# A transformer block on one core: the first norm modulated by halves of d, and a new order of loads and work around it

## The chip, the cores and the metric

The kernel runs on one core of a Trainium2 chip. The core has these engines: TensorE for matrix products (PE in the rows; PEld is its weight load), VectorE (DVE), ScalarE (ACT), GpSimd (POOL), and SyncE (SP), which here issues every DMA on one queue. They run side by side and wait for each other with semaphores. The metric is the time of one execution on the device in microseconds (us), as a median of several runs.

## The reference

The block has a modulated layer norm, a linear layer with a block mask, a gated residual, a second modulated norm, and a gated feed-forward net with 4-bit weights.

```python
mod = (silu(c) @ wmod).reshape(4, 6, 1, 1024)
sa, ca, ga, sb, cb, gb = (mod[:, i] for i in range(6))
ga, gb = ((2 * (g >= 0) - 1) * maximum(abs(g), 0.25) for g in (ga, gb))
h = layernorm(x) * (1 + ca) + sa                # x: (4, 512, 1024)
x = x + ga * (h @ (weight * block_mask).T)      # blocks of 32 x 32, any mask entry > 0 keeps one
h = layernorm(x) * (1 + cb) + sb
x = x + gb * ((silu(h @ w1.T) * (h @ w2.T)) @ w3.T)   # w1, w2: 2752 x 1024, w3: 1024 x 2752
```

All of it is in float32. A product is made of three TensorE products of rounded parts: high x high, high x low, low x high.

## The kernel before

The 2048 rows of x are 16 tiles of 128. The program is written by hand as one list of instructions for each engine, with explicit semaphore waits; nothing reorders them. So an instruction that waits holds up all that stands behind it in its engine's list, DMA issues on SP too.

The stage that the change touches is the first: modulation, the first norm, the masked layer, called attention in the names.

- **Modulation.** `modulation(j)` multiplies silu(c) with piece j of wmod (2 MB each, 12 pieces, 3 buffers; load j waits until piece j - 3 is used). Pieces 0 and 1 give row set 0 (the shift sa), 2 and 3 give row set 1 (the scale ca), 4 and 5 the gate ga, 6 to 11 the second norm's. `copy_rows` (ACT) takes a row set out of PSUM, `turn_mod` (PE) transposes it, `read_mod` (DVE) stores it as per-partition factors.
- **Masks and weights.** The weight matrix and the mask come in four pieces of 1 MB: pieces 0 and 1 are the two halves of d (the contraction) for output columns 0 to 511, 2 and 3 those for columns 512 to 1023. `sum_mask`, `mask_column`, `sum_partitions` (PE), `block_mask` make a mask of blocks for an output half. `mask_weight` on DVE (pieces 1 and 3) or POOL (0 and 2) applies it, `weight_high` (ACT) rounds the high part, `split_weight` (DVE) takes the low part and counts `w_lo`.
- **A tile.** `ln1_sums` and `ln1_factors` (DVE, a root on ACT) give mean and deviation, `norm1` (ACT) the normed tile, `turn1` (PE) transposes it in eight 128 x 128 pieces, `input1` (ACT) modulates the eight pieces and rounds the high part AH, `low_part1` (DVE) takes the low part AL. `attend_half(t, hb)` multiplies tile t with output half hb in 24 products of 512 columns. Then `residual_sum` and `residual_norm` (DVE) gate, add and norm again. For tiles 0 and 1 `set_aside` copies the product out first, because the gate isn't there yet: `gate(0)` (DVE) makes it from pieces 4 and 5, SP stores it to DRAM and loads it back spread over the partitions.
- **x slots.** Tile 5 goes into the slot of tile 1, so its load waits until tile 1's sum is stored; on SP it stands behind the store of tile 1's second norm.
- **Early decode.** ACT decodes the first feed-forward weights between tiles, four lines of 1024 columns at a time (`early_lines`).

PE's list is: mask sums, modulations 0 to 3, `turn1(0)`, `turn1(1)`, WARM = 24 products of the identity matrix (their result is not used), output half 0 of tiles 0 and 1, modulations 4 and 5, output half 1 of tile 0, then tile by tile, with `turn1(t + 1)` ahead of tile t's products. Modulations 6 and 7 stand behind tile 1.

## Time and profile before

| | before |
|---|---|
| median of 3 runs | 1596.86 us (1596.29 to 1597.66) |
| profiled execution | 1598.67 us, its span 1596.6 us |
| PE busy | 1547.7 us, 97% of the span |
| PE weight loads | 1272.2 us, 80% |
| DVE, ACT, POOL busy | 1040.9, 985.9, 10.6 us |
| chain that ended last, by engine | PE 93%, DVE 2%, DMA 2%, ACT 1% |

The profiled execution is one run on its own; its span runs from the first to the last instruction. In a timeline row the bracket names how long the engine had been idle ahead of it, and who ended that. PE busy counts the modelled length of overlapping products, so 97% says that PE was hardly without work and not that it ran at its peak. PEclk is the granted clock of TensorE as a share of 2.4 GHz: it is 1.00 or 0.50 (1.2 GHz), and between them only where a stretch holds both. Some products appear as two records (the 24 warm-up products as x48, a modulation as x32).

### The profile page before, as it was taken

Reading aid. Unit: us, or ns where it says so; the run is one execution under the profiler, and the core shown is the slowest. Engines: PE = TensorE matmul, PEld = TensorE weight load, DVE = VectorE, ACT = ScalarE, POOL = GpSimd, SP = SyncE. Lnnn points to the kernel's source line nnn. Section 1 sums busy time; section 2 is a strip of 40 time slices with the busy share of each in tenths; the row PEclk is TensorE's granted clock in tenths of the full one; section 3 lists DMA queues with packets and bytes.
Section 4 is the critical chain, followed back from the end, with each engine's and each line's share of the span. In section 5 each row is a group of like instructions: output and inputs, shape, how many; then the busy total and the mean of one; then the engine's idle time right before and its main releaser. Section 6 shows DMA issues by size and latency. Waiting matters only on the chain.

```text
span 1596.6 us, 19163 instructions
## 1 busy us (share of the span) xinstructions
PE 1547.7 (97%) x7216; PEld 1272.2 (80%) x7216; DVE 1040.9 (65%) x1496; ACT 985.9 (62%) x1280; POOL 10.6 (1%) x11
## 2 busy tenths in 40 slices
PE   3889999999999999999999999999999999999998
PEld 1667788888888888888888888888888888888887
DVE  3677787555455555456776666666775757867777
ACT  1445666899888888885698978887333433333320
POOL 1100000000000000000000000000000000000000
PEclk9899999999999999999999999999999999999999
DMA  9874521465555544553577777686777958958866
GB/s 369 326 260 156 185 83 64 166 208 178 185 178 166 183 158 158 170 165 125 192 236 224 239 223 237 199 243 185 262 273 267 348 192 301 337 194 300 308 217 208
DMA packets 170091, 345.97 MB, mean 217 GB/s; under 512 B 14728, under 2 KB 65288, under 8 KB 170000
## 3 DMA queue, kind: packets, MB, share of 16 engines
q1 hardware_dynamic: 170000, 344.76, 64.1%
q8 instruction: 57, 0.93, 0.2%
q14 instruction: 34, 0.28, 0.1%
HBM read 249.77 MB, written 94.93 MB: 216 GB/s over the span
## 4 chain that ended last, share of the span: by engine, by line
PE 93%; DVE 2%; DMA 2%; ACT 1%; issue 1%; SPq 0%; DVEq 0%; ACTq 0%
PE ps L1811 10%; PE ps L1813 10%; PE ps L1812 10%; PE ps L1886 9%; PE ps L1885 9%; PE ps L1884 9%; PE ps L1823 9%; PE ps L1822 9%; PE ps L1824 9%; PE ps L1746 3%; PE ps L1747 3%; PE ps L1748 3%; DMA wmod<-wmod 2%; PE ps L1710 2%; PE ps L1693 1%; ACT modulated L867 1%
## 5 line engine op out<-in xcount | busy, mean ns | idle before, releaser
L824 ACT ACTIVATE w_raw<-w_raw 128x1024 f32<-128x1024 f32 x287 | 304.8, 1062 | 9.1
L1811 PE MATMUL ps<-ffn_in_hi,w_hi 128*128 128x512 f32 x688 | 268.6, 390 | 0.0
L1813 PE MATMUL ps<-ffn_in_hi,w_lo 128*128 128x512 f32 x688 | 267.8, 389 | 0.0
L1812 PE MATMUL ps<-ffn_in_lo,w_hi 128*128 128x512 f32 x688 | 267.7, 389 | 0.0
L1884 PE MATMUL ps<-t_hi,s_hi 128*128 128x512 f32 x616 | 239.6, 389 | 0.0
L1885 PE MATMUL ps<-t_lo,s_hi 128*128 128x512 f32 x616 | 239.6, 389 | 0.0
L1886 PE MATMUL ps<-t_hi,s_lo 128*128 128x512 f32 x616 | 239.6, 389 | 0.0
L1822 PE MATMUL ps<-x_m_hi,stream_hi 128*128 128x512 f32 x604 | 235.0, 389 | 0.0
L1823 PE MATMUL ps<-x_m_lo,stream_hi 128*128 128x512 f32 x604 | 235.0, 389 | 0.0
L1824 PE MATMUL ps<-x_m_hi,stream_lo 128*128 128x512 f32 x604 | 235.0, 389 | 0.0
L1043 ACT ACTIVATE s_hi<-s_raw 128x1408 fp32r<-128x1408 f32 x56 | 77.5, 1383 | 230.6 <-DVE s_raw L1541 190.0
L836 ACT ACTIVATE w_raw<-w_raw 128x1024 f32<-128x1024 f32 (+1 forms) x154 | 163.4, 1061 | 4.4
L1101 DVE SCALAR_TENSOR_TENSOR w_raw<-w_raw,w_scale 128x1024 f32<-128x1024 f32 x41 | 50.3, 1226 | 174.9 <-ACT w_raw L824 174.9
L1813 PEld LDWEIGHTS ps<-ffn_in_hi,w_lo 128*128 128x128 f32 x688 | 129.1, 188 | 27.1
L1812 PEld LDWEIGHTS ps<-ffn_in_lo,w_hi 128*128 128x128 f32 x688 | 129.2, 188 | 26.5
L1811 PEld LDWEIGHTS ps<-ffn_in_hi,w_hi 128*128 128x128 f32 x688 | 129.2, 188 | 26.4
L1885 PEld LDWEIGHTS ps<-t_lo,s_hi 128*128 128x128 f32 x616 | 115.6, 188 | 24.2
L1884 PEld LDWEIGHTS ps<-t_hi,s_hi 128*128 128x128 f32 x616 | 115.6, 188 | 23.9
L1886 PEld LDWEIGHTS ps<-t_hi,s_lo 128*128 128x128 f32 x616 | 115.6, 188 | 23.9
L1822 PEld LDWEIGHTS ps<-x_m_hi,stream_hi 128*128 128x128 f32 x604 | 113.4, 188 | 23.7
L1824 PEld LDWEIGHTS ps<-x_m_hi,stream_lo 128*128 128x128 f32 x604 | 113.4, 188 | 23.5
L1823 PEld LDWEIGHTS ps<-x_m_lo,stream_hi 128*128 128x128 f32 x604 | 113.4, 188 | 23.4
(134 smaller groups left out, 2100.4 us busy)
## 6 DMA issues: line engine op xcount, KB each, us to landing
s_raw<-h_d SPq DMA_DIRECT2D x96, 704.0 KB, 5.5
stream_raw<-t_d SPq DMA_DIRECT2D x150, 256.0 KB, 3.5
t_d<-combined SPq DMA_DIRECT2D x106, 256.0 KB, 2.6
wmod<-wmod SPq DMA_DIRECT2D x12, 2048.0 KB, 16.3
t_raw<-w_d SPq DMA_DIRECT2D x88, 256.0 KB, 6.4
w_codes<-w12q SPq DMA_DIRECT2D x41, 512.0 KB, 5.1
h_d<-h_tile SPq DMA_DIRECT2D x44, 256.0 KB, 2.4
h_d<-up_c SPq DMA_DIRECT2D x44, 256.0 KB, 3.3
```

The costliest lines, as they stand in the source:

```text
L824: act.activation(RAWF[r], RAWF[r] if j else RQ[r][:], ACT.Prelu, bias=bias, scale=sign, alpha=slope).then_inc(line_ready, 1)
L836: act.activation(E3[p][0:rows, :], (E3 if j else E3Q)[p][0:rows, :], ACT.Prelu, bias=bias, scale=sign, alpha=slope).then_inc(w3_line, 1)
L1043: act.activation(SH[p][:], SR[p][:, 1], ACT.Copy).then_inc(s_hi, 1)
L1811: pe.matmul(acc, RH[r][:, k, :], HH[:, b, k, :], start=(k == 0), stop=False)
L1812: pe.matmul(acc, RH[r][:, k, :], HL[:, b, k, :], start=False, stop=False)
L1813: last = pe.matmul(acc, RL[r][:, k, :], HH[:, b, k, :], start=False, stop=(k == C - 1))
L1822: pe.matmul(acc, th[:, k, :], xh[:, k, :], start=(first and k == 0), stop=False)
L1823: pe.matmul(acc, th[:, k, :], xl[:, k, :], start=False, stop=False)
L1824: last = pe.matmul(acc, tl[:, k, :], xh[:, k, :], start=False, stop=(stop and k == HALF_C - 1))
L1884: pe.matmul(acc, SH[p][:, k, :], TH[place(i)][k][:], start=(k == 0), stop=False)
L1885: pe.matmul(acc, SH[p][:, k, :], TL[place(i)][k][:], start=False, stop=False)
L1886: last = pe.matmul(acc, SL[p][:, k, :], TH[place(i)][k][:], start=False, stop=(k == HC - 1))
```

## The change

What it does:

- The columns of wmod for sa and ca are sorted anew on the host: modulation pieces 0 and 1 now give shift and scale for the first half of d (row set 0), pieces 2 and 3 for the second (row set 1). `read_mod` writes two parts for each.
- Tiles 0 and 1 are turned, modulated, rounded and multiplied by halves of d: `half_turn1`, `half_input1`, `half_low_part1`, `attend_first`. A part is 12 products. Each waits for its weight piece and its half of the input.
- The loads stand in another order: mask pieces 0 and 1, modulation 0 and 1, weight 0, modulation 2 and 3, weight 1, masks 2 and 3, weights 2 and 3, then x tiles 2 and 3, modulation 4 and 5. The early decode's load waits for all four weight pieces in place of two.
- Masks 2 and 3 are summed behind the inputs of the first two tiles. DVE applies the mask to pieces 0, 1 and 2, POOL to piece 3 alone.
- Norms of tiles 2, 3 and 4 stand together ahead of the loop; `gate(0)` stands behind `set_aside(1)`; modulations 6 and 7 behind tile 2. WARM is 16.

`whole(t)` in the diff is t - 1, since tiles 0 and 1 no longer count on the tile semaphores; `weight_at(j)` is j + 1.

```diff
-                    sp.wait_ge(w_lo, 2)
+                    sp.wait_ge(w_lo, 4)
...
-            for j in range(4):
-                load_mask(j)
-            for j in range(3):
-                load_wmod(j)
+            load_mask(0)
+            load_mask(1)
+            load_wmod(0)
+            load_wmod(1)
             load_weight(0)
+            load_wmod(2)
             load_wmod(3)
-            for j in range(1, 4):
-                load_weight(j)
-            load_wmod(4)
-            load_wmod(5)
+            load_weight(1)
+            load_mask(2)
+            load_mask(3)
+            load_weight(2)
+            load_weight(3)
             sp.wait_ge(mask_step, MASK_STEPS + 2)
             load_x(2)
             load_x(3)
+            load_wmod(4)
+            load_wmod(5)
             load_x(EXTRA)
             load_wmod(6)
             load_early(0)
...
-            for j in (0, 2):
-                pool.wait_ge(mask_step, MASK_STEPS * (j // 2 + 1))
-                pool.wait_ge(weight_loaded[j], 16)
-                w4, m4 = masked_views(j)
-                pool.tensor_tensor(w4, w4, m4, ALU.mult).then_inc(piece_masked[0], 1)
+            pool.wait_ge(mask_step, 2 * MASK_STEPS)
+            pool.wait_ge(weight_loaded[3], 16)
+            w4, m4 = masked_views(3)
+            pool.tensor_tensor(w4, w4, m4, ALU.mult).then_inc(piece_masked[0], 1)
...
+            def half_input1(half, t):
+                e = 2 * half + t
+                cs = slice(HALF_C * half, HALF_C * (half + 1))
+                act.wait_ge(half_turned, 2 * t + half + 1)
+                if t:
+                    act.wait_ge(half_low1, e)
+                for c in range(HALF_C * half, HALF_C * (half + 1)):
+                    ins = act.activation(HM[0][:, c, :], ps[:, 4 + half, (c % 4) * P:(c % 4 + 1) * P], ACT.Identity,
+                                         bias=MODS[0][:, batch_of(t), c:c + 1], scale=MODS[0][:, batch_of(t), C + c:C + c + 1])
+                ins.then_inc(half_modulated1, 1)
+                act.wait_ge(half_modulated1, e + 1)
+                act.activation(AH[t][:, cs, :], HM[0][:, cs, :], ACT.Copy).then_inc(half_high1, 1)
...
+            act.wait_ge(mod_read, 2)
+            half_input1(0, 0)
+            half_input1(0, 1)
             copy_rows(1)
             weight_high(1)
-            act.wait_ge(mod_read, 2)
-            input1(0)
-            input1(1)
+            act.wait_ge(mod_read, 4)
+            half_input1(1, 0)
+            half_input1(1, 1)
             weight_high(2)
             weight_high(3)
             for t in range(TILES):
                 if t == 1:
+                    start1(3)
                     input1(2)
-                    start1(3)
+                    start1(4)
+                    input1(3)
                     root(1, 0)
...
+                    elif t > 2 and t + 1 < TILES:
...
-                if t + 2 < TILES and t != 1:
+                if t + 2 < TILES and t not in (1, 2):
...
+            def half_low_part1(half, t):
+                cs = slice(HALF_C * half, HALF_C * (half + 1))
+                dve.wait_ge(half_high1, 2 * half + t + 1)
+                dve.tensor_tensor(AL[t][:, cs, :], HM[0][:, cs, :], AH[t][:, cs, :].bitcast(F32), ALU.subtract).then_inc(half_low1, 1)
...
+            mask_weight(0)
+            read_mod(0)
+            split_weight(0)
+            half_low_part1(0, 0)
+            half_low_part1(0, 1)
+            mask_weight(1)
+            read_mod(1)
+            split_weight(1)
+            half_low_part1(1, 0)
             sum_mask(2)
+            half_low_part1(1, 1)
             sum_mask(3)
             mask_column(1)
             block_mask(1)
-            read_mod(0)
-            mask_weight(1)
-            split_weight(0)
-            read_mod(1)
-            split_weight(1)
-            low_part1(0)
-            mask_weight(3)
-            low_part1(1)
+            mask_weight(2)
             split_weight(2)
             split_weight(3)
...
+            ln1(2)
+            ln1(3)
+            set_aside(0)
+            low_part1(2)
+            set_aside(1)
+            gate(0)
+            ln1(4)
+            low_part1(3)
+            residual_sum(0)
+            residual_norm(0)
+            for t in range(2, TILES):
+                residual_sum(t - 1)
+                if 2 < t < TILES - 2:
+                    ln1_sums(t + 2)
...
+            def half_turn1(half, t):
+                pe.wait_ge(normed1, t + 1)
+                if t:
+                    pe.wait_ge(half_modulated1, 2 * half + 1)
+                for c in range(HALF_C * half, HALF_C * (half + 1)):
+                    last = pe.transpose(ps[:, 4 + half, (c % 4) * P:(c % 4 + 1) * P],
+                                        XN[t][:].rearrange("t (p c) -> t c p", c=C)[:, c, :], IDENT[:])
+                last.then_inc(half_turned, 1)
...
+            half_turn1(0, 0)
+            half_turn1(1, 0)
             modulation(0)
             modulation(1)
             turn_mod(0, 0)
+            for _ in range(WARM):
+                pe.matmul(ps[:, 2, 0:P], IDENT[:], IDENT[:], start=True, stop=True)
+            half_turn1(0, 1)
+            attend_first(0, 0, 0)
             modulation(2)
+            attend_first(1, 0, 0)
             modulation(3)
             turn_mod(1, 1)
-            turn1(0)
-            for t in range(TILES):
-                if t == 0:
-                    turn1(1)
-                    for _ in range(WARM):
-                        pe.matmul(ps[:, 7, 0:P], IDENT[:], IDENT[:], start=True, stop=True)
-                    pe.wait_ge(w_lo, 2)
-                    attend_half(0, 0)
-                    attend_half(1, 0)
-                    modulation(4)
-                    modulation(5)
-                    pe.wait_ge(w_lo, 4)
-                    attend_half(0, 1)
-                else:
-                    if t + 1 < TILES:
-                        turn1(t + 1)
-                    if t in (4, 7):
-                        turn_mod(t // 3 + 2, t // 3 + 1)
-                    if t > 1:
-                        attend_half(t, 0)
-                    attend_half(t, 1)
-                for j in {1: (6, 7), 5: (8, 9), 8: (10, 11)}.get(t, ()):
+            half_turn1(1, 1)
+            attend_first(0, 0, 1)
+            attend_first(1, 0, 1)
+            sum_partitions(1)
+            attend_first(0, 1, 0)
+            attend_first(0, 1, 1)
+            turn1(2)
+            attend_first(1, 1, 0)
+            attend_first(1, 1, 1)
+            modulation(4)
+            modulation(5)
+            for t in range(2, TILES):
+                if t + 1 < TILES:
+                    turn1(t + 1)
+                if t in (4, 7):
+                    turn_mod(t // 3 + 2, t // 3 + 1)
+                attend_half(t, 0)
+                attend_half(t, 1)
+                for j in {2: (6, 7), 5: (8, 9), 8: (10, 11)}.get(t, ()):
...
+    first = a["L0_wmod"][:, :2 * D].reshape(D, 2, P, 2, C // 2).transpose(0, 3, 2, 1, 4).reshape(D, 2 * D)
```

`attend_first(t, hb, half)` waits for `w_lo` of piece 2 * hb + half and for that half's low part, and issues the 12 products of it.

PE's list, from its start to the first attention products. `wmod` is a modulation piece, `normed_186` and `normed_187` are tiles 0 and 1, the products of `identity` alone the warm-up. Before:

```order
L1757 MATMUL ps<-mask_column,four_partition_groups 128x16 x2
L1693 MATMUL ps<-wmod_57,silu_c 4x256 x16
L1693 MATMUL ps<-wmod_58,silu_c 4x256 x16
L1702 MATMUL ps<-identity,mod_rows_193 128x4 x8
L1693 MATMUL ps<-wmod_59,silu_c 4x256 x16
L1693 MATMUL ps<-wmod_57,silu_c 4x256 x16
L1702 MATMUL ps<-identity,mod_rows_193 128x4 x8
L1710 MATMUL ps<-identity,normed_186 128x128 x8
L1710 MATMUL ps<-identity,normed_187 128x128 x8
L1772 MATMUL ps<-identity 128x128 x24
L1746 MATMUL ps<-attn_w_hi,attn_in_hi_78 128x512
```

Now, to the first attention product:

```order
L1829 MATMUL ps<-mask_column,four_partition_groups 128x16
L1770 MATMUL ps<-identity,normed_186 128x128 x8
L1744 MATMUL ps<-wmod_57,silu_c 4x256 x16
L1744 MATMUL ps<-wmod_58,silu_c 4x256 x16
L1753 MATMUL ps<-identity,mod_rows_193 128x4 x8
L1838 MATMUL ps<-identity 128x128 x16
L1770 MATMUL ps<-identity,normed_187 128x128 x4
L1804 MATMUL ps<-attn_w_hi,attn_in_hi_78 128x512
```

Tile 0 is turned ahead of the modulations, half of tile 1 behind the warm-up, and the attention products begin ahead of modulations 2 and 3.

DVE's list around the second output half. `mask_piece_62` and `_63` are masks 2 and 3, `weight_piece_66` and `_67` weights 2 and 3. Before:

```order
L1279 TENSOR_REDUCE mask_column<-mask_sums 128x16
L1284 TENSOR_SCALAR block_mask<-ps 128x16
L1272 TENSOR_REDUCE mask_sums<-mask_piece_62 128x4x16
L1272 TENSOR_REDUCE mask_sums<-mask_piece_63 128x4x16
L1279 TENSOR_REDUCE mask_column<-mask_sums 128x16
L1284 TENSOR_SCALAR block_mask<-ps 128x16
L1142 TENSOR_SCALAR mod_352<-ps 128x4x8
L1290 TENSOR_TENSOR weight_piece_65<-weight_piece_65,block_mask 128x2048
L1294 TENSOR_TENSOR attn_w_lo<-weight_piece_64,attn_w_hi 128x4x512
L1142 TENSOR_SCALAR mod_352<-ps 128x4x8
L1294 TENSOR_TENSOR attn_w_lo<-weight_piece_65,attn_w_hi 128x4x512
L1211 TENSOR_TENSOR attn_in_lo_80<-modulated_188,attn_in_hi_78 128x1024
```

Now:

```order
L1343 TENSOR_TENSOR attn_w_lo<-weight_piece_65,attn_w_hi 128x4x512
L1256 TENSOR_TENSOR attn_in_lo_80<-modulated_188,attn_in_hi_78 128x512
L1321 TENSOR_REDUCE mask_sums<-mask_piece_62 128x4x16
L1256 TENSOR_TENSOR attn_in_lo_81<-modulated_188,attn_in_hi_79 128x512
L1321 TENSOR_REDUCE mask_sums<-mask_piece_63 128x4x16
L1328 TENSOR_REDUCE mask_column<-mask_sums 128x16
L1333 TENSOR_SCALAR block_mask<-ps 128x16
L1339 TENSOR_TENSOR weight_piece_66<-weight_piece_66,block_mask 128x2048
L1343 TENSOR_TENSOR attn_w_lo<-weight_piece_66,attn_w_hi 128x4x512
L1343 TENSOR_TENSOR attn_w_lo<-weight_piece_67,attn_w_hi 128x4x512
```

The mask sums of pieces 2 and 3 moved from ahead of all weights to between and behind the low parts of the second half of d, and the mask of piece 2 is applied here.

ACT's list from the norm of tile 3 on. `x_184` is tile 3, `x_extra` tile 4, `modulated_188` with `attn_in_hi` an input of attention, `std` a root, `early_decoded` the early decode. Before:

```order
L855 ACTIVATE std_367<-var_eps_363 128x1
L862 ACTIVATE normed_187<-x_184,neg_mean_rstd_383,rstd_fine_385 128x1024
L855 ACTIVATE std_368<-var_eps_364 128x1
L867 ACTIVATE modulated_188<-ps,mod_352 128x128 x8
L880 ACTIVATE attn_in_hi_79<-modulated_188 128x1024
L855 ACTIVATE std_369<-var_eps_365 128x1
L855 ACTIVATE std_366<-var_eps_362 128x1
L862 ACTIVATE normed_186<-x_extra,neg_mean_rstd_382,rstd_fine_384 128x1024
L845 ACTIVATE early_decoded<-early_codes 128x1024
L845 ACTIVATE early_decoded<-early_decoded 128x1024 x3
L867 ACTIVATE modulated_188<-ps,mod_352 128x128 x8
L880 ACTIVATE attn_in_hi_78<-modulated_188 128x1024
```

Now:

```order
L869 ACTIVATE std_367<-var_eps_363 128x1
L878 ACTIVATE normed_187<-x_184,neg_mean_rstd_383,rstd_fine_385 128x1024
L883 ACTIVATE modulated_188<-ps,mod_352 128x128 x8
L911 ACTIVATE attn_in_hi_78<-modulated_188 128x1024
L869 ACTIVATE std_366<-var_eps_362 128x1
L878 ACTIVATE normed_186<-x_extra,neg_mean_rstd_382,rstd_fine_384 128x1024
L883 ACTIVATE modulated_188<-ps,mod_352 128x128 x8
L911 ACTIVATE attn_in_hi_79<-modulated_188 128x1024
L869 ACTIVATE std_368<-var_eps_364 128x1
L869 ACTIVATE std_369<-var_eps_365 128x1
L859 ACTIVATE early_decoded<-early_codes 128x1024
L859 ACTIVATE early_decoded<-early_decoded 128x1024 x3
```

The norm of tile 4 moved ahead of the input of tile 3, and the early decode stands right behind the two roots of the second norm.

## Rows read from the trace of the kernel before

**Rows 1.** The timeline of PE: start us, us, engine, line, operation, count, idle before and its releaser.

```profile
22.77 3.59 PE L1693 MATMUL ps<-wmod,silu_c 128*4 128x256 f32 x32 [0.77 <-DMA wmod<-wmod]
...
46.83 1.04 PE L1702 MATMUL ps<-identity,mod_rows 4*128 4x4 f32 x8 [1.67 <-ACT mod_rows L911]
...
61.62 0.48 PE L1746 MATMUL ps<-attn_w_hi,attn_in_hi 128*128 128x512 f32 x1
...
72.71 3.64 PE L1693 MATMUL ps<-wmod,silu_c 128*4 128x256 f32 x64
...
111.38 1.97 PE L1710 MATMUL ps<-identity,normed 128*128 128x128 f32 x8 [6.86 <-ACT normed L862]
```

**Rows 2.** The chain of waits that ended last: start us, us, what.

```profile
54.56 7.31 PE ps L1772 x48
...
115.91 0.43 PE ps L1746
...
116.73 0.23 PE ps L1748
...
125.85 0.88 PE ps L1710 x8
```

**Rows 3.** Windows of PE: stretch, us, PE busy (x), PEclk, DMA share, GB/s.

```profile
48.00:49.00 1.00, 1.00 (x7) 0.64 1.05 410
```

**Rows 4.** The timeline of ACT (ScalarE), first attention inputs and weights.

```profile
31.49 1.54 ACT L911 ACTIVATE mod_rows<-ps 4x256 f32<-4x256 f32 x4 [19.39 <-PE ps L1693]
...
39.48 1.91 ACT L916 ACTIVATE attn_w_hi<-weight_piece 128x2048 fp32r<-128x2048 f32 x1 [6.45 <-POOL weight_piece L803]
...
49.56 2.91 ACT L867 ACTIVATE modulated<-ps,mod 128x128 f32<-128x128 f32 x8 [0.91 <-PE ps L1710]
...
52.50 1.06 ACT L880 ACTIVATE attn_in_hi<-modulated 128x1024 fp32r<-128x1024 f32 x1
```

**Rows 5.** The timeline of DVE (VectorE), masks, weights, first low parts.

```profile
10.74 4.47 DVE L1272 TENSOR_REDUCE mask_sums<-mask_piece 128x64 f32<-128x2048 int32 x2
...
16.38 0.18 DVE L1284 TENSOR_SCALAR block_mask<-ps 128x16 f32<-128x16 f32 x1 [0.76 <-PE ps L1757]
...
44.41 2.29 DVE L1290 TENSOR_TENSOR weight_piece<-weight_piece,block_mask 128x2048 f32<-128x2048 f32 x1 [10.06 <-DMA weight_piece<-wT]
...
54.47 1.21 DVE L1211 TENSOR_TENSOR attn_in_lo<-modulated,attn_in_hi 128x1024 fp32r<-128x1024 f32 x1
```

**Rows 6.** The timeline of POOL (GpSimd), all of its work on weights.

```profile
35.81 3.64 POOL L803 TENSOR_TENSOR weight_piece<-weight_piece,block_mask 128x2048 f32<-128x2048 f32 x1 [33.07 <-DMA weight_piece<-wT]
...
47.23 5.17 POOL L803 TENSOR_TENSOR weight_piece<-weight_piece,block_mask 128x2048 f32<-128x2048 f32 x1 [7.79 <-DMA weight_piece<-wT]
```

**Rows 7.** The timeline of DVE, the split of weight piece 1.

```profile
48.92 5.62 DVE L1294 TENSOR_TENSOR attn_w_lo<-weight_piece,attn_w_hi 128x2048 fp32r<-128x2048 f32 x1
```

**Rows 8.** The timeline of DVE, norms of x tiles, gate, residual of tile 0, low part.

```profile
66.02 0.69 DVE L1175 BATCH_NORM_STATS2 stats<-x 128x6 f32<-128x512 f32 x1
...
76.41 1.71 DVE L1159 COPY gate<-ps 4x256 f32<-4x256 f32 x4 [7.40 <-PE ps L1693]
...
80.84 1.21 DVE L1168 SCALAR_TENSOR_TENSOR gate<-gate_sign,gate 4x1024 f32<-4x1024 f32 x1
...
92.17 1.22 DVE L1252 TENSOR_TENSOR normed_again<-normed_again,attn_gate 128x1024 f32<-128x1024 f32 x1
...
97.52 0.81 DVE L1266 TENSOR_SCALAR normed_again<-x,mean_var,rstd_fine 128x1024 f32<-128x1024 f32 x1
...
119.47 1.23 DVE L1211 TENSOR_TENSOR attn_in_lo<-modulated,attn_in_hi 128x1024 fp32r<-128x1024 f32 x1 [3.61 <-ACT attn_in_hi L880]
```

**Rows 9.** The timeline of ACT, a norm, a root, early decode.

```profile
69.05 1.25 ACT L862 ACTIVATE normed<-x,neg_mean_rstd,rstd_fine 128x1024 f32<-128x1024 f32 x1 [1.07 <-DVE neg_mean_rstd L1206]
...
96.44 0.20 ACT L855 ACTIVATE std<-var_eps 128x1 f32<-128x1 f32 x1 [4.04 <-DVE var_eps L1181]
...
124.35 4.32 ACT L845 ACTIVATE early_decoded<-early_decoded 128x1024 f32<-128x1024 f32 x4
```

132 lines of the change are left out of this document (71 added, 61 removed).

## The prediction

> **What bounds the kernel now.** I read the timeline of PE first. From 61.62 us, where the attention products start, PE is nearly always busy (busy for 97% of the span, by the page's table above), so only the start and the waits behind it can be gained. The reader is to see two things in [rows 1]: modulation can't start before its rows land at 22.77 us, and PE sits idle for 6.86 us before the transposes of tile 4 at 111.38 us. The chain of waits [rows 2] puts the transposes of tile 5 at 125.85 us. There both kernels will have done the same PE work (modulations 0 to 7, attention of tiles 0 to 3), and from there their order is the same. So the whole change is worth the difference at that point: 125.85 us, with the clock at its upper level (2.4 GHz), against the time at which the changed kernel gets there.
>
> The clock belongs to the sum. After the idle 6.86 us the eight transposes took 1.97 us [rows 1], against 0.88 us at 125.85, and an attention product took 0.43 us until 116.73, then 0.23 [rows 2]. A restart after a long gap thus costs 116.7 - 111.4 = 5.3 us at half speed, 2.65 us of work. The clock also falls in a merely sparse stretch: it went down between 48 and 49 us [rows 3], with only the 1.04 us transposes of 46.83 and a wait of 1.67 us ahead of them [rows 1] shortly before.
>
> **Part 1, loads.** The cumulative megabytes ahead of a load tell its arrival, since the queue was always full: 7 MB had landed at 22.77 us [rows 1], 12 MB at 35.81 [rows 6], 15 MB at 44.41 [rows 5]. By the new order modulation piece 1 (7 MB) comes at 22.8, weight piece 0 (8 MB) at 25.4, modulation pieces 2 and 3 (10 and 12 MB) at 30.6 and 35.8, weight piece 1 (13 MB) at 38.7, mask pieces 2 and 3 by 44.4. x tiles 2 and 3 and modulation pieces 4 and 5 now queue on SP behind the sum of mask piece 3 (about 55 us below). That is 5 MB, some 14 us at these rates, so the last lands at 69, and is needed at 82: hidden. If it came 13 us later, it would cost one for one.
>
> **Part 2, the first half of d.** Modulation 1 ends at 22.8 + 3.6 = 26.4 (x32, 3.59 us in [rows 1]); ACT copies rows 1.54 us, ScalarE's other prices are 1.91 us for a weight piece, 2.91 us for eight modulates, 1.06 us for their high part [rows 4]. From these a half takes 1.46 + 0.63 us (the copy by the line through 1.06 us at 1024 and 1.91 at 2048 columns). DVE's prices are 2.23 us for a mask sum, 2.29 for a weight piece, 1.21 for a low part [rows 5], so about 0.7 for a half's. Then: rows copied 28.0, turned 29.1, read 29.5, ACT's high weight 29.9, half input 0 at 32.0, its low part 32.9. PE meanwhile runs 16 warm-up products (24 took 7.31 us [rows 2], so 5.0 us) and half a turn: 34.6. Twelve products at 0.228 us (48 from 61.62 to 72.71 took 11.0 [rows 1]) are 2.75 us, and a modulation at the upper clock is 1.8 us (two in 3.64 [rows 1]): 37.3, 39.1, 41.9 and, with modulation 3, 43.7 us. Before it ended at 45.2 (46.83 less its wait of 1.67 [rows 1]). The pieces from 26.4 to 43.7 are now bound by PE, and no more by the loads.
>
> **Part 3, the second half of d.** Rows copied 45.2, turned 46.3, read 46.7; ACT's high weight 47.1; DVE's split 49.5; low part of tile 0 at 50.2. Only then can the next 24 products run, after 6.5 us with some 1.5 us of PE work in it, so I take them at half speed for 5.3 us: 24 x 0.228 + 2.65 = 8.1 us, to 58.3. If the clock held it would be 55.7. DVE's two mask sums, two low parts and the column (2.2 + 0.7 + 2.2 + 0.4) end at 55.8 and are hidden there. The mask product and block mask take 0.76 + 0.18 us [rows 5]: 59.3.
>
> **Part 4, the second output half.** This is what is moved back: before, all four mask pieces were summed in one go ahead of any weight. Now nothing of it can start before 59.3. DVE masks piece 2 (to 61.5) and POOL piece 3. POOL took 3.64 us at 35.81, and 5.17 from 47.23 to 52.40, with DVE at work beside it [rows 6]; the DVE split recorded from 48.92 took 5.62 instead of 2.3, to 54.5, that is 2.1 us after POOL was done [rows 7]. So these two take turns. DVE is first by its place (it makes the block mask itself): POOL to 65.2, and the split of piece 2, ready from ACT at 63.5, runs after POOL, to 67.4. PE waits for it from 59 to 67, and restarts cold. Then 24 products 8.1 (to 75.5), turn of tile 2 0.9, 24 products at full speed 5.5, modulations 4 and 5 3.6: **85.5 us**, where before they ended at 76.35 (72.71 + 3.64 [rows 1]). Tile 2's norm (split of piece 3 to 69.7, then 4.3 us by 66.02 to 70.3 [rows 8, 9]) is ready at 74.0 and hidden.
>
> The Trainium skill (SBUF — State Buffer, Who interferes with whom) says that a VectorE instruction with two SBUF inputs and a GpSimd one that reads SBUF lock each other out for the whole instruction, whichever starts first. The rows above agree, and it leaves open who starts first, which is the first rival.
>
> **Part 5, what is gained back, and where it goes.** PE goes on: turn, tile 2 (10.9), modulations 6 and 7 (3.6), turn, tile 3 (10.9): 27.3 us, to 112.8. For tile 5's turn it needs this chain from 85.5: gate 5.65 (76.41 to 82.05 [rows 8]); tile 4's norm on DVE and ACT 4.3; input of tile 3 4.0 and its low part 1.2 (15.2 so far; the gate's way through DRAM was over at the latest 15.8 us after modulation 5, at 92.17 [rows 8], so it costs 0.6 at most and I take none); residual of tile 0 6.16 (92.17 to 98.33 [rows 8]); the sums of tile 1 to ACT's root 4.5 (92.17 to 96.64 [rows 8, 9]); four lines of the early decode 4.3 [rows 9]; input of tile 4 4.0; from its low part to the end of tile 5's norm 5.0 (119.47 to 124.4 [rows 8, 9]). Sum 39.2: **124.7 us**. The 6.86 us before tile 4 go, but a wait of about 12 us before tile 5 takes their place. The restart is cold: 124.7 + 2.65 = 127.4, against 125.85. The sum is **+1.5 us**. Against the profiled execution's own 1598.67 that is 1600.2; the median of the runs shown is 1.8 us lower, and I forecast in its terms: 1596.86 + 1.5 = **1598.4**.
>
> **Rivals.** (a) POOL is first at 59.3: it ends at 62.9, DVE masks piece 2 to 65.2, ACT's high part is done at 67.1, the split at 69.3, all 1.9 us later: +3.4, 1600.3 us. It decides if POOL's operation starts before DVE's. For it: both wait for the same count. Against it: DVE gives that count itself. This is the slower side. (b) The clock holds, or comes back at once, in the two restarts at 50.2 and 67.4: each 2.65 us earlier, so 1598.4 - 5.3 = 1593.1. For it: the gap between 43.7 and 50.2 is broken by transposes. Against it: the fall in [rows 3] came in such a stretch, and the gap of 8 us is longer than the 6.86 us after which the restart was cold. (c) Tile 5's norm is not late: something in the 39.2 us overlaps that I have in a row (the early decode, the residuals). Then the turn follows at 112.8 with a warm clock, 13 us before 125.85: 1583.8. Against it: each piece is in order on its engine, and 11.9 us would have to go. (d) The change doesn't do what it says, since the first products stay behind the loads or ACT's copies: they would start well after 34.6. Each microsecond is then lost one for one, since the chain hangs on modulation 3; at 5 us late it is 1603.4. Against it: the full queue [rows 1, 5, 6] gives the arrivals.
>
> **How the numbers follow.** Forecast 52%, (a) 25%, (b) 10%, (c) 8%, (d) 5%. What a measurement of this kernel can tell from no change is about 0.2%, 3.2 us. The unknown sizes are the lengths of the cold stretches (one was measured, 5.3 us; I allow 2.6 us either way for each, so 1.3 us of work) and the hops between engines; they put the forecast's own range at 1595.5 to 1601.5, partly over the bound of 1600.1. Faster: (b), (c) and an edge, 20%. Slower: (a), (d) and an edge of the forecast, 31%. Same: 49%. The range from (b) to past (a) leaves out (c) and (d): 1593.3 to 1602.5.
>
> **What would show it.** First attention products at 34 to 35 us; modulation 3 done near 43.7; a PE wait for the split weight of about 8 us until 67; modulation 5 done near 85.5; no wait before tile 4's turn and one of 10 to 13 us before tile 5's, at about 124.7, with half speed behind it. A last modulation before 82 or after 89 would break part 3 or 4; a tile 5 turn without a wait would break part 5 and the forecast with it.

## The result, and the profile after

| | before | changed | forecast |
|---|---|---|---|
| median | 1597.57 us (1596.29 to 1598.54, 6 runs) | 1604.10 us (1602.65 to 1604.56, 6 runs) | 1.5 us over before |
| profiled execution | 1598.67 us, span 1596.6 | 1603.84 us, span 1601.8 | 1600.2 us |
| DVE, ACT, POOL busy | 1040.9, 985.9, 10.6 us | 1044.0, 986.5, 5.5 us | |
| end of modulation 5 | 76.35 us | 85.42 us | 85.5 us |
| turn of tile 5 | 125.85 us | 128.28 us | 124.7 us |

The changed kernel is slower: the ratio is 1.0040 (95% interval 1.0029 to 1.0051), 6.5 us in the medians and 5.2 us between the two profiled executions, where I had forecast 1.5 us. 1604.1 us is 5.7 us over the forecast time of 1598.4 us (0.7 of these because the first three runs of before had a median of 1596.86) and lies outside the range of 1593.3 to 1602.5 us. Up to its 85th microsecond the changed kernel ran nearly as the prediction says; then it lost 3.6 us more, in one place.

The timeline of PE in the changed kernel answers [rows 1 and 2]. L1804 is the first attention product of a run of 12 or 24, L1744 a modulation, L1770 half a turn, L1761 a whole turn.

```profile
22.77 1.91 PE L1744 MATMUL ps<-wmod,silu_c 128*4 128x256 f32 x32 [1.14 <-DMA wmod<-wmod]
...
32.96 0.48 PE L1804 MATMUL ps<-attn_w_hi,attn_in_hi 128*128 128x512 f32 x1
...
40.70 1.91 PE L1744 MATMUL ps<-wmod,silu_c 128*4 128x256 f32 x32
...
49.09 0.76 PE L1804 MATMUL ps<-attn_w_hi,attn_in_hi 128*128 128x512 f32 x1 [0.30 <-DVE attn_in_lo L1256]
...
56.24 0.29 PE L1829 MATMUL ps<-mask_column,four_partition_groups 128*128 128x16 f32 x2
66.93 0.79 PE L1804 MATMUL ps<-attn_w_hi,attn_in_hi 128*128 128x512 f32 x1 [10.40 <-DVE attn_w_lo L1343]
...
81.78 3.64 PE L1744 MATMUL ps<-wmod,silu_c 128*4 128x256 f32 x64
...
100.92 1.16 PE L1761 MATMUL ps<-identity,normed 128*128 128x128 f32 x8
...
128.28 1.97 PE L1761 MATMUL ps<-identity,normed 128*128 128x128 f32 x8 [15.29 <-ACT normed L878]
...
143.68 1.04 PE L1761 MATMUL ps<-identity,normed 128*128 128x128 f32 x8
```

The reader is to see that attention starts 28.7 us sooner (32.96 against 61.62), that the wait before tile 4's turn is gone (100.92 has no bracket, [rows 1] had 6.86 us), and that two waits stand in its place: 10.40 us for the weights of the second output half, and 15.29 us before the turn of tile 5.

The last line is the turn of tile 6. Before, it is

```profile
138.67 1.04 PE L1710 MATMUL ps<-identity,normed 128*128 128x128 f32 x8
```

that is 5.0 us sooner. From this turn to the end of the span it is 1457.9 to 1458.2 us in all fourteen profiles of this document, whatever the variant. So the whole difference between two profiled executions is made ahead of tile 6's turn, and can be read there.

Who holds that turn back is in the chain of waits (start us, us, what):

```profile
108.94 9.04 DMA x_d<-x
...
118.00 3.59 DMA x<-x
...
121.62 0.69 DVE stats L1219
...
126.98 1.25 ACT normed L878
```

The sum of tile 1 is ready at 108.93 (DVE's residual, L1307). Its store `x_d` takes 9.04 us to land, only then may tile 5 be loaded into that slot (3.59 us), and its statistics begin at 121.62. DVE had nothing else to do and waited 4.74 us for this load (its timeline, below). Part 5 of the prediction has neither the store nor the load.

What stands ahead of that slow store is in SP's timeline of DMA issues. Before:

```profile
98.72 0.43 SPq L428 DMA_DIRECT2D wmod<-wmod  x1
104.22 0.32 SPq L514 DMA_DIRECT2D x_d<-x  x1
109.18 0.32 SPq L519 DMA_DIRECT2D xn_d<-normed_again  x1
109.54 0.43 SPq L522 DMA_DIRECT2D x<-x  x1
```

In the changed kernel:

```profile
106.92 0.43 SPq L439 DMA_DIRECT2D wmod<-wmod  x1
108.94 0.32 SPq L529 DMA_DIRECT2D x_d<-x  x1
112.63 0.32 SPq L534 DMA_DIRECT2D xn_d<-normed_again  x1
118.00 0.33 SPq L537 DMA_DIRECT2D x<-x  x1
```

The order is the same in both, so the order of the lists could not show this. What changed is the distance. Modulation piece 9 (2 MB) used to be issued 5.5 us ahead of tile 1's store, now 2.0 us, since DVE's residuals of tiles 0 and 1 stand back to back (the low part of tile 3 used to run between them, and runs ahead of both now). That the small store is held up by the large load is so far a reading; the first experiment tests it. The DMA engines had no time to spare: from 108 to 118 us their busy share was 0.88 or more in every window. The load of tile 5 was issued at once before (0.36 us after the store ahead of it), and 5.4 us after it now.

The clock after that wait, in windows of PE (stretch, us, PE busy with its count, PEclk, DMA share, GB/s):

```profile
116.00:118.00 2.00, 0.00 (x0) 0.84 0.98 401
118.00:120.00 2.00, 0.00 (x0) 0.50 0.61 152
...
134.00:136.00 2.00, 2.00 (x10) 0.89 0.66 240
```

PE went idle at 112.99 with the granted clock at 2.4 GHz, it fell to 1.2 GHz between 116 and 118, and stayed there until 134.5, some 6.2 us past the restart.

DVE's timeline, the second output half's mask and split, tile 0's residual and tile 5's statistics, answering [rows 5, 7 and 8]:

```profile
56.57 0.17 DVE L1333 TENSOR_SCALAR block_mask<-ps 128x16 f32<-128x16 f32 x1 [2.02 <-PE ps L1829]
56.84 5.76 DVE L1339 TENSOR_TENSOR weight_piece<-weight_piece,block_mask 128x2048 f32<-128x2048 f32 x1
64.58 4.49 DVE L1343 TENSOR_TENSOR attn_w_lo<-weight_piece,attn_w_hi 128x2048 fp32r<-128x2048 f32 x2 [1.98 <-ACT attn_w_hi L950]
...
100.36 1.22 DVE L1301 TENSOR_TENSOR normed_again<-normed_again,attn_gate 128x1024 f32<-128x1024 f32 x1
...
121.62 0.69 DVE L1219 BATCH_NORM_STATS2 stats<-x 128x6 f32<-128x512 f32 x1 [4.74 <-DMA x<-x]
```

And POOL's, answering [rows 6]:

```profile
56.83 3.64 POOL L817 TENSOR_TENSOR weight_piece<-weight_piece,block_mask 128x2048 f32<-128x2048 f32 x1 [54.10 <-DVE block_mask L1333]
```

POOL starts 0.01 us ahead of DVE, runs its 3.64 us undisturbed, and DVE's 2.29 us become 5.76, ending 2.13 us after POOL. That is rival (a) of the prediction. The profile calls its spans on POOL rough, so the 0.01 us alone would be thin; but the 2.13 us behind POOL's end are about what DVE's product takes undisturbed.

### The profile page after: what moved, and what is told of

It reads as the page before. It is cut to its first block, busy times and chain, and to the rows that moved or that the text cites. A ratio compares the mean times of both kernels' runs of the same rounds, so it can differ in the third digit from the quotient of the medians.

```text
span 1601.8 us, 19147 instructions
## 1 busy us (share of the span) xinstructions
PE 1545.7 (96%) x7200; PEld 1272.1 (79%) x7200; DVE 1044.0 (65%) x1501; ACT 986.5 (62%) x1282; POOL 5.5 (0%) x10
## 4 chain that ended last, share of the span: by engine, by line
PE 92%; DVE 3%; DMA 2%; ACT 1%; issue 1%; SPq 0%; DVEq 0%; ACTq 0%
PE ps L1888 10%; PE ps L1887 10%; PE ps L1886 10%; PE ps L1960 9%; PE ps L1959 9%; PE ps L1961 9%; PE ps L1897 9%; PE ps L1899 9%; PE ps L1898 9%; PE ps L1804 3%; PE ps L1805 3%; PE ps L1806 3%; PE ps L1761 2%; DMA wmod<-wmod 1%; PE ps L1744 1%
## 5 line engine op out<-in xcount | busy, mean ns | idle before, releaser
L1140 DVE SCALAR_TENSOR_TENSOR w_raw<-w_raw,w_scale 128x1024 f32<-128x1024 f32 x41 | 50.2, 1225 | 175.1 <-ACT w_raw L838 175.1
```

## The experiments

My theory after the result (A): 3.6 us of the miss are the load of tile 5 behind piece 9's, the rest of the loss is what the prediction says, the second output half's mask coming late. The rival (B): tile 5's norm is late through DVE and ACT anyway, and the load only fills time that they would have taken. Ratios are to the kernel before, timed beside each.

Two things limit what the sizes below can say. Each ratio has an interval of about 0.1% either way, 1.6 us, so a step of 3 us between two medians is known to 2 us or so. And each variant has one profiled execution, and these differ in their first 50 us by up to 1.8 us for no edit's sake: the first product of the second half of d starts at 49.09 in the changed kernel, at 50.90 with piece 9 early, at 50.44 with the masks sooner, and at 49.30 in a kernel with both edits. So I read an edit's effect in a trace from the last common point ahead of it.

**Piece 9 loaded earlier.**

```diff
             load_ga(batch_of(0))
+            load_wmod(9)
...
-                if t in (0, 1, 5):
-                    load_wmod({0: 9, 1: 10, 5: 11}[t])
+                if t in (1, 5):
+                    load_wmod({1: 10, 5: 11}[t])
```

> Changed kernel with one DMA moved on SP: modulation piece 9 (2 MB) is issued right behind the load of the gate, and no longer between the stores of tiles 0 and 1. Theory A (the store of tile 1 took 9.0 us because it stood behind piece 9 on the queue, and the load of tile 5 waits for that store): the store lands by about 112 us, the load of tile 5 is issued near 113, right behind the store of tile 1's second norm at 112.6, and is there near 116.7; tile 5's turn on PE comes at 124 to 125 us in place of 128.3, and the time is 3.5 us below the changed kernel's, near 1600.5. Rival B (the store is slow by itself, or tile 5's norm is held by the chain through the early decode and the input of tile 4 anyway): the load is issued near 118 again, or the turn stays within 1 us of 128, and the time stays near 1604.

Measured: 1600.00 us (1599.32 to 1602.70, 10 runs), ratio 1.0017 (1.0008 to 1.0027). SP's issues now:

```profile
110.00 0.32 SPq L530 DMA_DIRECT2D x_d<-x  x1
...
114.04 0.43 SPq L538 DMA_DIRECT2D x<-x  x1
```

The store has landed by the time that SP asks, and the load goes out 4.0 us after the store instead of 9.1. Piece 9 (issued at 100.38) now stands 3.5 us ahead of the store of tile 0, on which no load waits. PE:

```profile
82.84 3.64 PE L1745 MATMUL ps<-wmod,silu_c 128*4 128x256 f32 x64
...
125.27 1.97 PE L1762 MATMUL ps<-identity,normed 128*128 128x128 f32 x8 [11.22 <-ACT normed L879]
```

From modulation 5's end (86.48; this execution was 1.1 us later there) to tile 5's turn it is 38.8 us, against 42.9 in the changed kernel and 39.2 in the prediction's sum. So theory (A) holds for the missing link, worth 4.1 us by this and by the medians (3.7 by the ratios), and the prediction's chain is right once the link is taken out: it describes this kernel, not the one it was made for.

**No POOL in the second output half.** POOL's product is taken out, DVE applies the mask to piece 3 too.

```diff
-            pool.wait_ge(mask_step, 2 * MASK_STEPS)
-            pool.wait_ge(weight_loaded[3], 16)
-            w4, m4 = masked_views(3)
-            pool.tensor_tensor(w4, w4, m4, ALU.mult).then_inc(piece_masked[0], 1)
...
             mask_weight(2)
+            mask_weight(3)
             split_weight(2)
```

> Changed kernel with the mask of weight piece 3 put on by DVE behind that of piece 2; POOL does nothing there. Theory A (POOL's 3.64 us held up DVE's mask of piece 2, which took 5.76 us for 2.29): piece 2 is masked by 59.1 us in place of 62.6, piece 3 by 61.4, the low part of piece 2 is there by 63.7 in place of 66.9, PE goes on 3.2 us earlier, modulation 5 ends near 82.2, and since all up to tile 5's turn hangs on it, the time falls by 3.2 us, to about 1600.9. Rival B (the chain behind modulation 5 has its own start, or the clock eats it): below 1 us, near 1604.

Measured: 1600.79 us (1598.56 to 1603.48, 10 runs), ratio 1.0017 (1.0007 to 1.0026). DVE does both pieces in less time than one took beside POOL:

```profile
56.90 4.49 DVE L1332 TENSOR_TENSOR weight_piece<-weight_piece,block_mask 128x2048 f32<-128x2048 f32 x2
61.31 4.49 DVE L1336 TENSOR_TENSOR attn_w_lo<-weight_piece,attn_w_hi 128x2048 fp32r<-128x2048 f32 x2
```

The split starts 3.3 us sooner, modulation 5 ends 3.3 us sooner (82.08), and the median falls by 3.3 us. The second engine was a loss. The full agreement is in part luck: DVE waits 5.89 us for tile 5's load here, PE 16.4 us before its turn instead of 15.3, so that turn is only 2.2 us sooner (126.05) and tile 6's 1.2 us (142.50). The slow load is a cost of its own, and takes back part of what is won ahead of it.

**Products of the identity in both gaps**, 42 ahead of the second output half and 64 ahead of tile 5's turn, so that PE is hardly idle there. They move no work; only the clock can change.

```diff
             sum_partitions(1)
+            for _ in range(42):
+                pe.matmul(ps[:, 3, 0:P], IDENT[:], IDENT[:], start=True, stop=True)
...
+                if t == 4:
+                    for _ in range(64):
+                        pe.matmul(ps[:, 7, 0:P], IDENT[:], IDENT[:], start=True, stop=True)
```

> Changed kernel with identity products whose result is not used in the two long waits of PE: 42 before the first part of output half 1, 64 before tile 5's turn. Nothing else changes. Theory A (each long wait costs a restart at 1.2 GHz): the granted clock stays 1.00 in both places, the 24 products behind the first wait take 5.5 us in place of 8.4, tile 5's transposes take 1.0 us in place of 1.97, and the time falls by 2.9 + 2.6 = 5.5 us, to about 1598.6. Rival B (the clock costs nothing on the path, since PE waits for others anyway): the first part's gain is eaten by the gate's chain, at most 2.6 us in all, 1601.5 or more.

Measured: 1599.59 us (1598.82 to 1601.30, 10 runs), ratio 1.0012 (1.0002 to 1.0021), mean granted clock 0.998 instead of 0.986.

```profile
65.94 0.50 PE L1804 MATMUL ps<-attn_w_hi,attn_in_hi 128*128 128x512 f32 x1 [0.94 <-DVE attn_w_lo L1343]
...
126.03 1.16 PE L1761 MATMUL ps<-identity,normed 128*128 128x128 f32 x8 [1.65 <-ACT normed L878]
```

The first product takes 0.50 instead of 0.79 us and the turn 1.16 instead of 1.97. By the medians the two restarts at half speed cost 4.5 us together; the prediction has 5.3, and I had expected 5.5 here. By this trace it is less: tile 6's turn (139.15) is 4.5 us sooner, but the execution was 1.0 us ahead already at the block mask (55.74), which leaves 3.5. Tile 2's turn now waits 0.64 us for its norm and DVE 5.42 us for tile 5's load, so some of the gain is absorbed.

**The second output half's masks summed sooner**, mask 2 ahead of `read_mod(1)`, mask 3 ahead of tile 1's low part, and the mask product on PE ahead of tile 1's 12 products.

```diff
             mask_weight(1)
+            sum_mask(2)
             read_mod(1)
...
             half_low_part1(1, 0)
-            sum_mask(2)
-            half_low_part1(1, 1)
             sum_mask(3)
+            half_low_part1(1, 1)
...
-            attend_first(1, 0, 1)
             sum_partitions(1)
+            attend_first(1, 0, 1)
```

> Changed kernel with the sum of mask piece 2 moved on DVE ahead of the second reading of the modulation, that of piece 3 ahead of the last half low part, and on PE the mask product moved ahead of tile 1's second part. Theory A (the second output half starts when its block mask is there): the block mask comes near 54.4 us in place of 56.7, the first product of output half 1 near 64.6 in place of 66.9, modulation 5 ends near 83.1, and the time falls by about 2.3 us, to about 1601.8. Rival B (the mask piece isn't there yet at 42 us, and the sum holds up the reading of the modulation and the first two tiles): output half 0 ends 1 us or more later and the time stays at 1604 or rises.

Measured: 1601.25 us (1599.62 to 1603.62, 10 runs), ratio 1.0018 (1.0009 to 1.0028), 2.9 us under the changed kernel. The block mask ends at 55.33 instead of 56.74 us, though this execution was 1.35 us behind up to the second half of d: from its first product (50.44) to the block mask it is 4.9 us instead of 7.65, 2.8 us less, as the median has it. The late mask is thus a cost on the path, as part 4 says.

**The three edits together** (piece 9 early, no POOL, masks sooner):

> The changed kernel with the three edits of order together: modulation piece 9 behind the gate's load, all masks by DVE, masks summed earlier. Alone they gave 4.1, 3.3 and 2.9 us. Theory A (they are links of one chain, one behind the other: the block mask, the split of piece 2, modulation 5, the gate, the load of tile 5): they add up, modulation 5 ends near 80 us, tile 5's turn comes 38.5 to 39.5 us behind it, at about 119, and the time falls by 9 to 10 us from the changed kernel, to about 1594.5. Rival B (PE's own work is the next bound): PE has no wait before tile 5's turn, and the fall is smaller than 7 us.

Measured: 1592.97 us (1591.82 to 1594.67, 7 runs), ratio 0.9968 (0.9957 to 0.9979). Alone the edits gave 4.1, 3.3 and 2.9 us, 10.3 in all; together 11.1, which is the same within these intervals. PE:

```profile
118.05 1.97 PE L1756 MATMUL ps<-identity,normed 128*128 128x128 f32 x8 [11.34 <-ACT normed L875]
```

Modulation 5 ends at 79.15, and the turn comes 38.9 us later: the chain of part 5 again, the second time within 0.4 us of its sum. Now it is this chain of DVE and ACT that ends last, as rival (B) had it, with no DMA wait of more than 0.82 us in it.

**These three and the identity products** (16 and 48 of them):

> As the kernel with three edits of order, with 16 unused identity products in the shorter first wait (about 4 us) and 48 in the second (about 11.5 us). Theory A (each wait over some 5 us lets the clock fall, and the first two parts' stretch starts cold anyway): the second restart at full clock gives 2.6 us, the first at most 2.6, together 3 to 5 us below the kernel with three edits, 1590 to 1591.5. Rival B: the added products end later than what PE waits for and cost what they give: no difference.

Measured: 1591.36 us (1590.33 to 1592.16, 4 runs), ratio 0.9959 (0.9945 to 0.9974); the same kernel timed again beside the last variant below gave 1590.73 us (1590.43 to 1591.98, 5 runs), ratio 0.9958 (0.9945 to 0.9970). That is 1.6 to 2.2 us, less than the 3 to 5 I expected. In the second execution modulation 5 ends 1.5 us sooner (77.61), but DVE now waits 1.96 us for tile 5's load instead of 0.82, so the turn comes at 117.67 against 118.05: of the time won in front only 0.4 us are left, and the rest is the clock, which is up there: from the turn of tile 5 to that of tile 6 it is 13.1 us, against 15.5 with the three edits alone.

**The gate sooner.** The chain is now gate, norm of tile 4, input of tile 3, residuals. Piece 8's load moves behind the gate's store and load, so that these two meet an empty queue, and the norm of tile 4 ahead of the gate. One thing more differs from the kernel just shown: 34 identity products in the second wait instead of 48.

```diff
             load_wmod(7)
-            load_wmod(8)
...
             load_ga(batch_of(0))
+            load_wmod(8)
             load_wmod(9)
...
             low_part1(2)
+            ln1(4)
             set_aside(1)
             gate(0)
-            ln1(4)
```

> As the last kernel, and modulation piece 8's load moved behind the gate's way through DRAM, tile 4's norm on DVE moved ahead of the gate; 34 identity products in the second wait in place of 48. Theory A (the start of tile 0's residual hangs on the gate's landing and the low part of tile 3, both about 15 us behind modulation 5): the gate lands 12 us behind modulation 5, tile 5's turn comes about 36 us behind it in place of 39, and the time falls by another 3 us, to about 1587.5. Rival B (the store of the gate is slow by its own latency, or the next link, the load of tile 5, becomes late): less than 1 us.

Measured: 1593.15 us (1591.93 to 1594.17, 8 runs), ratio 0.9971 (0.9961 to 0.9982): no gain, 1.8 us more than without it. SP:

```profile
85.15 0.34 SPq L507 DMA_DIRECT2D gates_d<-gate  x1
86.90 0.36 SPq L510 DMA_DIRECT2D attn_gate<-gates_d  x1
87.30 4.74 SPq L439 DMA_DIRECT2D wmod<-wmod  x2
...
99.81 0.32 SPq L530 DMA_DIRECT2D x_d<-x  x1
...
106.59 0.33 SPq L538 DMA_DIRECT2D x<-x  x1
```

The gate's store landed in 1.75 us instead of 5.0, so that part worked. But pieces 8 and 9, 4 MB, now stand directly ahead of the stores: tile 1's store takes 6.8 us from issue, DVE waits 1.97 us for the store of tile 0's second norm and 1.12 us for tile 5's load. It is the changed kernel's fault made a second time, by my own hand. PE:

```profile
117.46 1.59 PE L1756 MATMUL ps<-identity,normed 128*128 128x128 f32 x8 [4.54 <-ACT normed L875]
```

That is 39.7 us behind modulation 5 (77.76), against 40.1 in both profiles of the kernel without the move, where I had expected 36. So the queue explains why nothing was won, but not the 1.8 us lost. Those are the clock's: PE waited 4.54 us behind the fewer identity products, the granted clock fell (0.51 from 118 to 120 us), and from this turn to tile 6's it took 15.8 us instead of 13.1.

**The same with the large loads spread**: piece 8 behind the gate's load, piece 9 behind tile 5's load, piece 10 behind tile 6's.

```diff
             load_wmod(8)
-            load_wmod(9)
...
-                if t in (1, 5):
-                    load_wmod({1: 10, 5: 11}[t])
+                if t in (1, 2, 5):
+                    load_wmod({1: 9, 2: 10, 5: 11}[t])
```

> As the kernel with the gate sooner, but with the loads of modulation pieces spread: piece 8 behind the gate's load, piece 9 behind the load of tile 5, piece 10 behind that of tile 6. In the kernel with the gate sooner pieces 8 and 9 stood together behind the gate's load, DVE waited 1.97 us for a store of tile 0 and 1.12 us for tile 5, and tile 5's turn came 39.7 us behind modulation 5. Theory A (those two waits were the queue's, and hid the gate's gain): they go, and tile 5's turn comes 36 to 37 us behind modulation 5; the time is 2.5 to 3 us below the kernel with three edits and warm-up products (1591.4), near 1588.7. Rival B (the loads only collide elsewhere, at tile 6): tile 6's turn waits 2 us or more, and the time is 1590.5 or higher.

Measured: **1587.79 us** (1587.47 to 1589.25, 5 runs), ratio 0.9941 (0.9928 to 0.9955), 2.9 us under the kernel timed beside it without these moves (its expectation:)

> The kernel with three edits and warm-up products once more, beside the last one on the same chip, with more rounds. It measured 1591.36 us against 1598.1 for the kernel before. Both theories expect 1591 to 1592, that is 0.4% below before; it is here for the comparison with the kernel with spread loads.

```profile
99.23 0.32 SPq L529 DMA_DIRECT2D x_d<-x  x1
...
103.28 0.43 SPq L537 DMA_DIRECT2D x<-x  x1
```

Tile 5's load goes out at once, and its turn is at

```profile
114.45 1.16 PE L1755 MATMUL ps<-identity,normed 128*128 128x128 f32 x8 [2.07 <-ACT normed L874]
```

in PE's timeline, 37.2 us behind modulation 5 (77.22) and with the clock up, though there are 34 identity products here too (tile 6's turn follows 13.1 us later). This is the fastest of all kernels here, 10.2 us under before and 16.3 under the changed one.

**Before, with its gap filled** by 28 identity products ahead of tile 4's turn:

```diff
+                    if t == 3:
+                        for _ in range(28):
+                            pe.matmul(ps[:, 7, 0:P], IDENT[:], IDENT[:], start=True, stop=True)
                     if t + 1 < TILES:
```

> The kernel before with 28 unused identity products in its own wait of 6.9 us ahead of tile 4's turn, nothing else. Theory A (the restart at 1.2 GHz behind that wait costs 5.3 us at half speed): the clock stays at 1.00, the eight transposes take 1.0 us in place of 1.97, and the time is 2.6 us below the kernel before, near 1595. Rival B (the next tile's chain on DVE absorbs it): within 0.5 us of before.

Measured: 1597.24 us (1596.05 to 1600.13, 10 runs), ratio 0.9998 (0.9989 to 1.0007): nothing that can be told from no change, where I expected 2.6 us. PE:

```profile
110.90 1.16 PE L1710 MATMUL ps<-identity,normed 128*128 128x128 f32 x8 [0.59 <-ACT normed L862]
...
124.00 1.16 PE L1710 MATMUL ps<-identity,normed 128*128 128x128 f32 x8 [1.02 <-ACT normed L862]
```

The clock was held, as the 1.16 us show against 1.97 [rows 1]. But tile 5's turn now waits 1.02 us for its norm, so it comes 1.85 us earlier than in [rows 2] and no more, and 0.45 of that this execution had won already at modulation 5 (75.90). The price of a cold restart, 2.65 us in the prediction, is what it costs only where nothing else is nearly as late.

**Before, with the new order of norms alone**: tile 3's norm ahead of the gate, tile 4's and tile 3's input ahead of the residuals (the low part of tile 3 behind tile 0's residual); loads, masks and weights as they were. In DVE's list (ACT's follows it):

```diff
                     ln1_factors(2)
+                    ln1_sums(3)
+                    ln1_factors(3)
                     gate(0)
...
-                    ln1_sums(3)
-                    ln1_factors(3)
+                    ln1_sums(4)
+                    ln1_factors(4)
                     set_aside(1)
...
                     residual_norm(0)
+                    low_part1(3)
```

> The kernel before with one part of the change alone: the norms of tiles 3 and 4 on ScalarE and VectorE come ahead of the input of tile 3, as in the changed kernel; loads, masks, weights, WARM and the first two tiles stay as before. (Tile 3's low part stands behind tile 0's second norm.) Theory A (the change has two parts of opposite sign: this one takes away the wait ahead of tile 4's turn and shortens the way from modulation 5 to tile 5's turn; the moved masks and loads end modulation 5 by 9 us later, which eats it): modulation 5 ends near 76.4 us, tile 4's turn has no wait, tile 5's turn comes 40 to 43 us behind modulation 5, at 117 to 119 in place of 125.9, and the time is 6 to 8 us below before, 1590 to 1592. Rival B (the new order of norms is itself what costs, by the load of tile 5 behind piece 9): 1596 or more.

Measured: 1596.39 us (1595.84 to 1597.46, 11 runs), ratio 0.9991 (0.9982 to 1.0000). A miss: I expected 1590 to 1592. SP shows why:

```profile
99.69 0.43 SPq L428 DMA_DIRECT2D wmod<-wmod  x1
102.85 0.32 SPq L514 DMA_DIRECT2D x_d<-x  x1
...
110.74 0.33 SPq L522 DMA_DIRECT2D x<-x  x1
```

Piece 9 is 3.2 us ahead of the store, not 5.5, and tile 5's load waits 3.9 us for it. The collision belongs to this part of the change, without any of the others. PE:

```profile
121.01 1.97 PE L1713 MATMUL ps<-identity,normed 128*128 128x128 f32 x8 [4.82 <-ACT normed L862]
```

The turn comes 44.2 us behind modulation 5 (76.78), where I expected 40 to 43. It is 4.7 us sooner than before all the same (125.69 in that timeline); but its restart is cold, and half of this is lost by tile 6's turn (136.36, 2.3 us sooner). The expectation, a turn 7 to 9 us sooner and a time 6 to 8 us lower, left too little for that restart.

**The same with piece 9 behind the gate's load** (the first experiment's edit):

> As the last kernel, with modulation piece 9's load right behind the gate's load and no longer between the stores of tiles 0 and 1. Theory A (the store of tile 1 stands behind piece 9 there too): tile 5's load is issued 3 us sooner, its turn comes 39 to 40 us behind modulation 5, and the time is 1 to 3 us below the last kernel, 1588.5 to 1590.5. Rival B (piece 9 now delays the stores, since it waits for modulation 6 and blocks the queue): no gain or a loss.

Measured: 1593.02 us (1592.25 to 1593.82, 6 runs), ratio 0.9969 (0.9957 to 0.9981). In PE's timeline the turn of tile 5 moves from 121.01 to

```profile
117.09 1.16 PE L1714 MATMUL ps<-identity,normed 128*128 128x128 f32 x8 [1.87 <-ACT normed L863]
```

The edit gives 3.4 us here (1 to 3 expected) and 4.1 in the changed kernel. The time is 2.5 us over the range expected (1588.5 to 1590.5), and here the trace says why. The turn itself is at full clock and 8.6 us sooner than before; but the granted clock fell right behind it (stretch, us, PE busy, PEclk, DMA share, GB/s):

```profile
117.00:118.00 1.00, 0.91 (x8) 1.00 0.97 397
118.00:119.00 1.00, 1.00 (x11) 0.77 0.65 115
119.00:120.00 1.00, 1.00 (x4) 0.50 0.75 250
```

It stayed down until 125.3 us, and tile 6's turn (133.08) comes 16.0 us behind tile 5's instead of 13.1, which leaves 5.6 of the 8.6 us. PE had waited only 1.87 us, with attention products back to back ahead of the wait. Behind waits of 1.65 to 2.07 us that followed identity products (four profiles above) the clock stayed up. So the length of a wait alone doesn't decide it, against what I expected with the identity products above, and no run here tells what does.

This splits the change. The order of norms alone, with the collision out of the way, makes the kernel before 4.8 us faster (1597.86 to 1593.02). All the rest of the change on top (1593.02 to 1600.00, with piece 9 early in both) costs 7.0 us, for all the 28.7 us that attention starts sooner: the halves of d with their loads, masks and weights, and also the gate behind `set_aside(1)`, modulations 6 and 7 behind tile 2 and the fewer warm-up products, which no run takes apart. With the masks sooner and without POOL it costs nothing and brings nothing: 1592.97.

## Why the prediction was wrong, point by point

- **The method** held: behind this stage the kernels run the same. The turns of tile 5 differ by 2.43 us (128.28 and 125.85), the second clock ramp adds some 2.65 by the prediction's price, 5.1 in all; at tile 6's turn the difference is 5.0, and the spans differ by 5.2. Tile 6's turn would have been the better point to compare, since it has the ramp behind it: from turn to turn it is 15.40 us in the changed kernel and 12.98 before, so the ramp cost 2.4.
- **Parts 1 and 2** (first products 34.6, modulation 3 done 43.7): 32.96 and 42.61. Early by 1.1 to 1.6 us, since modulation 1 took 1.91 us where I took 3.59 from [rows 1]. Before, modulations 0 and 1 took 3.59 and 3.54 us (at 22.77 and 27.88); in the changed kernel modulation 0 took 3.60 (at 18.02) and modulation 1 1.91. The granted clock can't show this, it reads 1.00 at all four. The transposes of tile 0 now stand ahead of the modulations, but whether they matter was not tested. Rival (d) is out.
- **Part 3** (second half's products 50.2 to 58.3, at half speed; block mask 59.3): 49.09 to 56.24, cold at its start (0.76 us for the first product), block mask at 56.74. The 24 products took 7.15 us instead of 8.1: the cold stretch was shorter than in the row I took it from. Rival (b) is out: every restart was cold.
- **Part 4** (split done for PE at 67.4, modulation 5 at 85.5): 66.93 and 85.42. This exactness is the luck of errors that cancel: the block mask 2.6 us early; POOL first, rival (a), late by the 1.9 us that its own sum gives and 0.2 us in the hops between engines; and 0.4 us more from there to modulation 5, most of it in the cold products (8.4 us for 8.1). The evidence that the count is given by DVE itself said nothing about which engine starts first.
- **Part 5** (tile 5's turn 39.2 us behind modulation 5, at 124.7): 42.9 us, at 128.28. This is the failed step. Its terms were right one by one: residual of tile 0 at 14.9 us behind modulation 5 (15.2 forecast), ACT's root of tile 1 at 110.71 (111.3 by the sum), input of tile 4 done at 119.03 (119.7). The sum lacks the load of tile 5, whose own chain runs from tile 1's residual through a store and a load of 9.04 and 3.59 us, and ended at 121.6, 4.7 us after DVE was free for it. The first experiment shows it: without that link the same stretch took 38.8 us, and the time fell by 4.1. The prediction counted DMAs where they were moved (x tiles 2 and 3, modulations 4 and 5) and not where engine work moved around them. Rival (c) is out.
- **The range** failed for the same reason. Its upper end, 1602.5, was rival (a) at 1600.3 and some spread; that norm 5 could come later still through a transfer was in no rival. (Its lower end, 1593.3, is 0.2 us above the 1593.1 of rival (b) that it was meant to hold.) The two profiled executions differ by 5.2 us, 3.7 more than forecast, and this link is 3.6 of them. In the medians the miss is 5.0 us; the other 1.4 are only that the profiled execution of before lay 1.1 us over its median, that of the changed kernel 0.3 us under its own.

The page on shared ports that the prediction cites, of the Trainium skill (SBUF — State Buffer, Who interferes with whom), is borne out to its last clause: one engine blocks the other for the whole instruction, 5.76 us for 2.29, and whoever starts first wins, by 0.01 us here.

What stays open: why the cold stretch at the start (7.15 us for 24 products) cost less than the later ones (8.4 behind the wait of 10.40 us), why the clock fell behind a wait of 1.87 us in one kernel, and whether a store behind a 2 MB load waits its turn or shares the bandwidth with it. Only the distances were tried, not a second queue.

## What to carry to other kernels

When a change moves compute work, write down for each slot that is loaded again the chain from the last use through the store to the next load, and the distance of these DMAs to the large ones ahead of them: the queue's order can be unchanged and its spacing not. Sum the chain to the wait that remains, and ask of each saved wait what is late next, loads included; here three of the gains (the gap of 6.86 us, the gate, the clock held up) each ended at a norm or a load that was nearly as late. Compare two kernels at a point behind the last cold restart: the same turn at full clock can be followed by a slow stretch. Two engines on one job are not faster if they take turns.
